# A gated cross-attention block on one core: batch 0's x in two loads, a reordered start, six warm-up matmuls

## What is computed

```python
memory_proj = einsum('bme,de->bmd', ctx, W_mem)
scores = einsum('bnd,bmd->bnm', x, memory_proj) / sqrt(D)
memory_context = einsum('bnm,bmd->bnd', softmax(scores), memory_proj)
gate = sigmoid(einsum('bnf,df->bnd', concat([x, memory_context]), W_gate) + b_gate)
x = rmsnorm(x + gate * memory_context) * norm_w
q = layernorm(x, g, b) @ Wq * scale;  k, v = split(ctx @ Wkv)      # 16 heads of 64
out = softmax(where(mask, q k^T, neg_inf)) v
x = x + tanh(attn_gate) * (out @ Wo)
x = x + tanh(ff_gate) * (gelu(layernorm(x, g2, b2) @ W1) @ W2)
```

## Time and profile before

| | |
|---|---|
| median of 3 runs | 209.27 us (209.02 to 211.89) |
| the profiled execution | 210.25 us, its span 208.4 us |
| PE busy | 202.4 us of the span (97%) |
| DVE, ACT, POOL busy | 148.0, 130.5, 71.3 us |
| moved | 10.06 MB, mean 48 GB/s over the span |

### The profile page before, as it was taken

One profiled execution on the slowest core, in us unless ns is written; L12 is line 12 of the kernel. 1 busy time (PEld: TensorE's weight loads), 2 busy tenths in 40 slices (PEclk: granted clock), 3 DMA queues, 4 the chain that ended last, 5 costly groups with the idle time before them and its releaser, 6 DMA issues.

```text
span 208.4 us, 4502 instructions
## 1 busy us (share of the span) xinstructions
PE 202.4 (97%) x1505; PEld 169.1 (81%) x1505; DVE 148.0 (71%) x529; ACT 130.5 (63%) x414; POOL 71.3 (34%) x71
## 2 busy tenths in 40 slices
PE   7999999999999999999999999999999999999993
PEld 3567868888689799787978988888886799988992
DVE  1779997779967698778698889997479673235310
ACT  4386757849766787665665838979996820168300
POOL 2010423853336244407140664685725006000000
PEclk9999999999999999999999999999999999999999
DMA  6995060050000000000000000015000001100001
GB/s 184 301 378 193 5 203 0 5 201 0 0 3 2 3 2 0 5 2 3 0 2 3 0 2 3 0 32 174 2 0 3 0 0 34 48 25 0 24 32 58
DMA packets 9297, 10.06 MB, mean 48 GB/s; under 512 B 1330, under 2 KB 8116, under 8 KB 9268
## 3 DMA queue, kind: packets, MB, share of 16 engines
q1 hardware_dynamic: 8468, 9.32, 13.4%
q10 hardware_dynamic: 800, 0.39, 0.6%
HBM read 8.66 MB, written 1.05 MB: 47 GB/s over the span
## 4 chain that ended last, share of the span: by engine, by line
PE 90%; DMA 4%; DVE 2%; SPq 2%; issue 0%
PE bank L513 57%; PE bank L1338 9%; PE bank L1310 8%; PE bank L1452 8%; DMA ctx_sb<-in_ctx_dram 4%; PE bank L1348 3%; PE bank L1293 2%; PE bank L1378 2%; SPq L560 2%; PE bank L1218 1%; PE bank L1231 1%; DVE wkv_lo L1069 1%; DVE x_sb L1171 0%; PE bank L1364 0%; DVE ctx_probsT_even L1014 0%
## 5 line engine op out<-in xcount | busy, mean ns | idle before, releaser
L630 POOL TENSOR_TENSOR probs<-expd,row_rcp 128x512 f32<-128x512 f32 x39 | 40.2, 1050 | 54.4 <-DVE row_rcp L1004 49.7
L760 ACT ACTIVATE expd<-expd,neg_max 128x128 f32<-128x128 f32 x128 | 49.6, 392 | 2.4 <-DVE neg_max L994 2.4
L994 DVE CUSTOM_DVE_ANT_0 expd<-bank,mask_bias 128x128 f32<-128x128 f32 x128 | 28.2, 286 | 2.2 <-PE bank L1310 2.1
L513 PE MATMUL bank<-xhT_pair,wq_pair 128*128 128x256 f32 x192 | 26.1, 289 | 0.0
L513 PE MATMUL bank<-wo_pair,oT_pair 128*128 128x256 f32 x192 | 26.0, 288 | 0.0
L513 PEld LDWEIGHTS bank<-xhT_pair,wq_pair 128*128 128x128 f32 x192 | 23.8, 191 | 2.0 <-issue 1.2
L760 ACT ACTIVATION_READ_ACCUMULATOR expd<-expd,neg_max 128x1 f32 x128 | 24.5, 191 | 0.0
L513 PEld LDWEIGHTS bank<-wo_pair,oT_pair 128*128 128x128 f32 x192 | 23.9, 190 | 0.5 <-issue 0.4
L513 PE MATMUL bank<-wq_pair,gelu_pair 128*128 128x256 f32 x192 | 23.6, 284 | 0.1
L513 PEld LDWEIGHTS bank<-wq_pair,gelu_pair 128*128 128x128 f32 x192 | 23.3, 192 | 0.5 <-DVE x_sb L1171 0.4
L1338 PE MATMUL bank<-ident,probs 128*128 128x128 f32 x160 | 21.1, 275 | 0.0
(11 more groups left out here) (163 smaller groups left out, 358.5 us busy)
## 6 DMA issues: line engine op xcount, KB each, us to landing
stage<-in_L_xattn_W_dram SPq DMA_DIRECT2D x2, 1024.0 KB, 5.2
x_sb<-in_x_dram SPq DMA_DIRECT2D x4, 256.0 KB, 6.4
wkv_sb<-in_L_xattn_Wkv_dram SPq DMA_DIRECT2D x2, 512.0 KB, 6.2
stage<-in_L_xattn_Wq_dram SPq DMA_DIRECT2D x1, 1024.0 KB, 9.9
stage<-in_L_xattn_Wo_dram SPq DMA_DIRECT2D x1, 1024.0 KB, 5.3
out_dram<-x_sb SPq DMA_DIRECT2D x8, 128.0 KB, 1.8
ctx_sb<-in_ctx_dram SPq DMA_DIRECT2D x4, 192.0 KB, 6.6
probs<-in_L_xattn_W_gate_dram SPq DMA_DIRECT2D x1, 512.0 KB, 9.0
```

The source lines that it names most:

```text
L513: last = nc.tensor.matmul(bank_ap, lhs(a), rhs(c), start=start and n == 0, stop=stop and n == 2)
L630: nc.gpsimd.tensor_tensor(probs[:, r, :].rearrange("p (h k) -> p h k", h=hb), expd[:, r, :].rearrange("p (h k) -> p h k", h=hb), row_rcp[: ...
L760: last = nc.scalar.activation(here, here, ACT.Exp, bias=neg_max[:, r, h:h + 1], scale=-1.0, accum_out=row_sum[:, r, h:h + 1])
L994: last = nc.vector.tensor_tensor_reduce(expd[:, r, h * w:(h + 1) * w], SC[n % 2][:, h * w:(h + 1) * w], mask_bias[:, first:first + w], -1. ...
```

## The change

1. x of batch 0 comes as two loads of one 128-token tile each, with a semaphore each; its transposes go tile by tile, in place of column half by column half.
2. SP issues the hot context tiles ahead of the values' weights.
3. Six warm-up matmuls in place of eight, with the same 512 columns, read from a 128-column operand four times over; DVE clears only that part.
4. The identity matmuls are 2, 1, 2, 3, 2 at five places, in place of 3, 2 at two.
5. `splitv` and `splito` on POOL go as instructions of 512 columns in place of 1024.
6. All four tables are in a new order.

```diff
-WARM_UP = 8
-DUMMIES = (3, 2)
+WARM_UP = 6
+DUMMIES = (2, 1, 2, 3, 2)
...
-    ("xT", 0), ("ctxT", 0), ("y", 0), ("tiles",), ("ctxT", "hot"), ("scores", "ctx", 0, 0), ("look", "PE"),
+    ("xT", 0), ("dummy", 0), ("ctxT", 0), ("dummy", 1), ("tiles",), ("dummy", 2), ("y", 0), ("look", "PE"),
...
-            load_x(0)
+            load(x_sb[:, 0, :], x[0, 0:P, :], x_in[0])
+            load(x_sb[:, 1, :], x[0, P:N, :], x0_rest_in)
             load(mask_tiles[:, :], mask.rearrange("b (t n) -> (b t) n", n=P), w_in["tiles"])
+            load(ctx_tiles[:, 1:B, HOT, :], ctx_in[1:B, HOT * P:M, :].rearrange("b p e -> p b e"), ctx_arrived[1])
             load(wkv_sb[:, INNER:2 * INNER], wkv[:, INNER:2 * INNER], w_in["wvalue"])
-            load(ctx_tiles[:, 1:B, HOT, :], ctx_in[1:B, HOT * P:M, :].rearrange("b p e -> p b e"), ctx_arrived[1])
...
-                        nc.gpsimd.tensor_tensor(wkv_lo[:, INNER:2 * INNER], wkv_sb[:, INNER:2 * INNER],
-                                                value_hi[:, :].bitcast(F32), ALU.subtract).then_inc(pool["kvlo"], 1)
+                        for half in (slice(0, BANK), slice(BANK, INNER)):
+                            of_kv = slice(INNER + half.start, INNER + half.stop)
+                            last = nc.gpsimd.tensor_tensor(wkv_lo[:, of_kv], wkv_sb[:, of_kv],
+                                                           value_hi[:, half].bitcast(F32), ALU.subtract)
+                        last.then_inc(pool["kvlo"], 1)
...
-            nc.vector.memset(warm, 0.0).then_inc(warm_ready, 1)
+            nc.vector.memset(warm[:, 0:P], 0.0).then_inc(warm_ready, 1)
...
-                        te.wait_ge(x_in[0], 16)
-                        for k in range(K):
-                            free(path, st, k)
-                            for t in range(T):
+                        for t in range(T):
+                            te.wait_ge((x_in[0], x0_rest_in)[t], 16)
+                            for k in range(K):
+                                if t == 0:
+                                    free(path, st, k)
...
-                nc.tensor.matmul(CONTEXT[:, :], warm[:, 0:P], warm[:, :], start=True, stop=True)
+                nc.tensor.matmul(CONTEXT[:, :].rearrange("p (a n) -> p a n", n=P), warm[:, 0:P],
+                                 warm[:, 0:P].rearrange("p (a n) -> p a n", a=1).to_broadcast([P, BANK // P, P]),
+                                 start=True, stop=True)
```

More of the change, by code:

```diff
@@ new lines @@
+    ("xT", 0), ("dummy", 0), ("ctxT", 0), ("dummy", 1), ("tiles",), ("dummy", 2), ("y", 0), ("look", "PE"),
+    ("branch", "PE"), ("ctxT", "hot"), ("scores", "ctx", 0, 0), ("dummy", 3), ("v", "hot", 0, 0), ("dummy", 4),
+    ("weights",), ("v", "hot", 0, 1), ("spread", "ctx", 0, 0), ("xT", 1), ("gatemem",), ("u", 0), ("k", "hot", 0),
+    ("ctxT", 1), ("k", "hot", 1), ("gate", 0), ("k", "hot", 2), ("k", "hot", 3), ("y", 1), ("v", "hot", 1, 0),
+    ("k", "hot", 4), ("scores", "ctx", 1, 0), ("k", "hot", 5), ("k", "hot", 6), ("xhT", 0), ("k", "hot", 7),
@@ new lines @@
+    ("v", "hot", 1, 1), ("xT", 2), ("spread", "ctx", 1, 0), ("q", 0, 0), ("u", 1), ("scores", "head", 0, 0),
+    ("q", 0, 1), ("q", 0, 2), ("scores", "head", 0, 1), ("gate", 1), ("scores", "head", 0, 2), ("v", "hot", 2, 0),
+    ("q", 0, 3), ("spread", "head", 0, 0), ("ctxT", 2), ("scores", "head", 0, 3), ("av", 0, 0), ("y", 2),
+    ("spread", "head", 0, 1), ("v", "hot", 2, 1), ("scores", "ctx", 2, 0), ("wo", 0, 0), ("xhT", 1), ("av", 0, 1),
+    ("v", "hot", 3, 0), ("spread", "head", 0, 2), ("q", 1, 0), ("q", 1, 1), ("scores", "head", 1, 0), ("av", 0, 2),
```

150 lines of the change are left out of this document (71 added, 79 removed), and 35 rows, old and new, of tables (SCALAR_ORDER, TENSOR_ORDER, VECTOR_ORDER).

## The result

| | kernel before | changed kernel |
|---|---|---|
| median of 6 runs | 209.37 us (209.02 to 211.89) | 212.14 us (211.58 to 214.41) |
| ratio | | 1.0134 [1.0101, 1.0167] |
| profiled execution: span | 208.4 us | 211.8 us |

The changed kernel is 2.8 us, or 1.3%, slower: less than the 2% that count as a change here, but clearly measured. The forecast was 210.8 us with a range of 208.4 to 213.0. The sign and the full range held; the median lies 1.3 us above the forecast, and above the forecast's own range of 209.9 to 211.3, so it is inside only because the range had been drawn out to the rivals.

What follows compares the result with a forecast made beforehand. TensorE's fixed row of stages bounds the kernel: +1.67 us for the start, -0.2 for exits, so +1.5 on the 209.27 median gives 210.8 us; own range 209.9 to 211.3, full range 208.4 to 213.0.

Steps and rivals of the forecast that it cites:

- The bound: TensorE, busy 97%, bounds the kernel; whatever delays the first keys' stage, at 17.93 us before, delays the end as much.
- The landing of the weights: Gate's weights' load: same data ahead, so their stage still starts at 13.81; one more issue adds at most 0.5 us.
- The stand and the three filling stages behind it: TensorE idles some 2.4 us before the weights; second values' stage and spread follow later, context tiles after keys: +1.67 us.
- The inputs' cover of 1.0 to 1.5 us: Values' copy and probabilities are ready 1.0 to 1.5 us before the second values' stage and spread need them.
- the walk: Summed ACT durations at the start: second exponential ends at 13.3, values' copy at 13.9, scaled probabilities there at 14.3.
- Two loads, hot tiles earlier, priced at 0: Start, before TensorE's standing time: split x and earlier hot tiles gain nothing at the end; price 0, up to 0.5.
- The long part, -0.2 for the exits: From the keys on: 21 in place of 22 exits from part-array stages, each costing 0.21 us, so -0.2.
- The named waits of the weight loads: Long part: weight loads waiting for other engines, some 4.6 us, worth 2 to 2.4 on TensorE; taken as equal.
- Warm-ups and dummies, price 0: Start: six warm-ups end at about 3.7 in place of 4.55, five more dummies lie in waits; price 0.
- a rise before the weights: Start: a clock that rises late but before 13.81 costs nothing, as the standing time absorbs it.
- The clock as a rival: TensorE's clock falls or rises late around the standing time: +1.65 us, 212.5, about 214 if twice as long; chance 0.13.
- The prediction's sign for it: A 512-column matmul taking 0.43 us behind the standing time would show the lower clock.

Runs made afterwards that it cites:

- after_again: The changed kernel run once more, unaltered, in the second group of timings: 213.35 us, ratio 1.0155.
- one_load: The changed kernel with x of batch 0 in one load again, waited for once: 211.69 us, ratio 1.0099.
- half_fill: The changed kernel with 14 in place of 2 identity matmuls at the last place, ahead of the gate's weights: 211.2 us, ratio 1.0057.
- fill_gap: The changed kernel with 24 in place of 2 identity matmuls at the last place, ahead of the gate's weights: 211.6 us, ratio 1.0089.
- v01_ahead: The changed kernel with the second values' stage moved ahead of the gate's weights on TensorE alone: 212.75 us, ratio 1.017.
- before_w_first: The kernel before with only the weights' stage and its copies moved ahead of second values' stage, context tiles and spread: 213.11 us, ratio 1.0148.
- start_restored: The changed kernel with the three filling stages back ahead of the weights on TensorE, ACT and DVE: 212.47 us, ratio 1.0114.
- eight_warm_ups: The changed kernel with eight warm-ups in place of six, in the new form: 211.37 us, ratio 1.0054.
- before_two_loads: The kernel before with x of batch 0 as two loads, both waited for before its transposes: 210.96 us, ratio 1.0061.
- new_long_part: The kernel before up to the first keys' stage and x of batch 1, then the changed kernel's new tables: 211.91 us, ratio 1.0093.
- restored_one_load: The changed kernel with the old start order before the gate's weights and x of batch 0 in one load: 212.3 us, ratio 1.0111.

## Why the prediction was right, and where it was not

**The bound, and the first keys' stage as the point that sets the end.** Right. From the first keys' stage to the start of DVE's last output (208.53 in the changed kernel) the profiles give 187.08 us for the kernel before, 186.95 for the changed one, and 186.96 for after_again, one_load, half_fill, fill_gap and v01_ahead, with starts of that stage anywhere from 18.82 to 21.58. In these the end follows that start one to one. It does not where DVE is late at the start as well: before_w_first and start_restored have 187.59.

**The landing of the weights "does not move".** Right within what the profiles can show. The weights' stage began at 13.81 before and at 13.99 and 14.18 in the two profiles of the changed kernel. The issue moved from 4.73 to 5.27, by 0.54, about the bound. But the landing does not follow the issue: in eight_warm_ups (second row) the load was issued 1.36 us later than in the changed kernel, and the stage began 0.80 us earlier.

```profile
5.27 1.35 SPq L560 DMA_DIRECT2D probs<-in_L_xattn_W_gate_dram  x1
```

```profile
6.63 0.49 SPq L560 DMA_DIRECT2D probs<-in_L_xattn_W_gate_dram  x1
```

The landing itself scatters more than the bound: where TensorE waited for it, the weights' stage began anywhere from 12.99 (v01_ahead) to 14.18, in profiles of kernels with the same data ahead of it. A single profile can't settle half a microsecond here.

**The stand and the three filling stages behind it, +1.67.** The mechanism was right, the size 0.2 high. The stages from the weights to the keys took 5.67 to 5.72 at the full clock; the sum of starts gave 5.90. u is where it was dear: put at 1.72, it takes 1.54 from start to start (20.04 to 21.58) when no longer followed by gatemem. That makes 5.70 less the 4.12 of the kernel before, less 0.11: 1.47. The full-clock spans rose by 1.6 in the second group and, for the first runs, by about 1.5 (209.1, against 209.37 less 1.8 outside the span); forecast +1.5. That the order costs this was also shown with the stand filled (209.4, 209.8).

**The inputs' cover of 1.0 to 1.5 us.** Right in its effect: no stage waited for ACT. In the profile after the second exponential's sum was read at 13.77 and the values' copy ran from 13.66 to 14.24, near the 13.3 and 13.9 of the walk:

```profile
13.57 0.20 ACT L760 ACTIVATION_READ_ACCUMULATOR expd<-bank,neg_max 128x1 f32 x1
13.66 0.58 ACT L817 COPY v_sb<-bank 128x512 f32<-128x512 f32 x1
13.98 1.04 POOL L631 TENSOR_TENSOR probs<-expd,row_rcp 128x512 f32<-128x512 f32 x1 [12.21 <-DVE row_rcp L1009]
```

```profile
13.99 1.31 DVE L1013 TENSOR_SCALAR probs<-expd,row_rcp 128x512 f32<-128x512 f32 x1
```

The probabilities were there at 15.02 from POOL and at 15.30 from DVE, not at 14.3. In a fall that is hidden. In two profiles without one the last of them was written at 14.49 (one_load) and 14.16 (half_fill), and the spread began at 15.34 and 15.11. So the cover was some 0.9 us, not 1.5.

**Two loads, hot tiles earlier, priced at 0.** Right in the changed kernel, by one_load, but for a reason the prediction had only in part. The second load alone cost the kernel before about a microsecond (before_two_loads). That loading the hot tiles first is what avoids this is argued from the profile and not shown by a run.

**The long part, -0.2 for the exits.** Not found. The stretch is shorter by 0.13, and 0.11 of that is the difference between the context tiles and x of batch 1, which changed sides. The named waits of the weight loads did not stay equal: they fell from 4.6 to 2.3 us, while those called "issue" rose from 10.2 to 11.7, and TensorE's own idle time rose by 0.26. That the length came out the same all the same is in part luck, and it holds for this start only (new_long_part, +1.9).

**Warm-ups and dummies, price 0.** Half right. The two missing warm-ups do not cause the falls. They can let the clock rise late: x's transposes took 0.60 in eight_warm_ups, but 0.90 in the profile of the changed kernel and 1.18 in after_again, which took up the full clock only within y. As the prediction said of a rise before the weights, this cost nothing at the end; the stand took it up. But something of their number moved the time outside the span: 2.63 us for the changed kernel, 1.8 for the kernel before, and 1.8 again with 8 warm-ups, or with 14 or 24 dummies ahead of the weights. That is +0.8 us that no step of the prediction had, because its sum was made on the span and took the rest as equal without a reason. It is the largest part of what the forecast missed. No profile shows this time. It goes neither with the loads (one_load 2.65) nor with the order of the start (start_restored 2.80). Over all kernels the number of warm-ups and dummies together goes with it, but not in one direction: 13 have 1.8, 16 have 2.4 to 2.8, and 18, 28 and 38 have 1.8. Its cause is open.

**The clock as a rival, at 0.13.** This term was mis-sized as a chance and not as a price. 5 of 12 executions had a fall, and their span was 2.1 to 2.7 us longer. The clock's own price is 1.7 of that (7.40 less 5.70), where the prediction gave 1.65. The rest fits a later landing; this is an estimate: from the keys to the end both kinds take the same, so a span of 209.1 puts the first keys' stage at 18.9 and the weights' stage at 13.2, against 21.58 and 14.18 in the fall that was profiled. The prediction's sign for it, a matmul of 512 columns that takes 0.43, could not have told the two levels apart: the two of the values' stage take 0.86 together at the full clock (10.01 to 10.87), and 1.56 in the fall. The Trainium skill ("TensorE: Matmul & The Clock Gate", the section on the clock gate) says that an idle stretch closes the gate; this case's traces agree, with matmuls at the lower clock behind stands of 3.08, 2.29, 2.19 and 1.97 us. Stands of 2.06 (before_w_first) and 1.45 (one_load) had none in five executions each, which is too few to say that they have none at all. The Trainium skill's remark on that page (the part on the PE-mode transpose) that transposes do not count as activity in the same way, which I had weighed against this change, is not borne out by these runs: in start_restored TensorE has nothing but transposes and the wait of 1.08 us from 12.55 to 16.53, restored_one_load is built the same way, and the two had no fall in 12 executions.

**The sum as it came out**, in medians: about +1.5 for the order, as forecast, +0.8 outside the span, and 0.4 for the falls, which reach the median only in part (212.14 with them, 211.7 for the four executions without). Together 2.8, rounded. So the mechanism and its size were right, and of the 1.3 us above the forecast 0.8 came from a place that the prediction had not looked at. That the full range held nevertheless is partly luck: its upper end had been drawn for the clock.

## What to carry to other kernels

A wait for a transfer that is covered by work which must be done anyway is free; moving that work behind the wait costs its full length, if the engine that does it is the bound. Such a stand has a second price on TensorE, in some executions only, since its clock may be lower behind it: look at the granted clock of every execution and not at one profile, and fill the stand with cheap matmuls if it can't be avoided (here 1.0134 and 1.0155 became 1.0057). An order of stages that was laid out for one start may not carry over to another, since the other engines' lists can be full at the same place, as DVE's was here; a filling stage goes back only together with its copies.

## What the runs showed of the hardware

- The clock was lower in 5 of 12 executions of one and the same kernel, and in 0 of 14 with the same stand filled. A fall made 8 transposes of 128 columns take 1.90 us in place of 1.09, and 2 matmuls of 512 columns up to 1.89 in place of 1.02. Where it set in differed too: at the weights' stage in the profile after, one stage later in eight_warm_ups.
- The granted clock in the profile does not show the slow start: it reads 1.00 from 0 to 6 us in the kernel before, where eight warm-ups take 0.44 us each, the lower level of 1.2 GHz. There the durations tell, and not the clock.
- With one load of 256 KB split into two of 128 KB, the hot tiles, further back in the same queue, landed so late that TensorE waited 2.24 us for them in the profile of before_two_loads; the keys' stage came 1.15 us later, and the full-clock span was 0.9 us longer.
- A 512 KB load issued at 6.63 us was there by 13.38, and one issued at 5.27 only by 14.18: with the same data ahead of it, the landing did not follow the issue.
- The time outside the span was 1.8 us for some programs and 1.9 to 3.2 (medians 2.4 to 2.8) for others with the same loads and nearly the same instructions. A change of a few tenths of a per cent can lie in there, where no profile shows it.
